# A fused early-fusion block on one core: softmax subtraction moved from GpSimd to VectorE, first-norm rows moved the other way, the attention steps written out

## What is computed

```python
h = concatenate([tok(x), txt], axis=1)            # 64 x 113 x 128
n = layernorm(h)                                  # "first norm"
q, k, v = split(n @ Wq, n @ Wkv)                  # 8 heads of 64
scores = einsum("bqhd,bkhd->bhqk", q * 0.125, k).astype(bfloat16)
probs  = softmax(scores)                          # bfloat16
h = h + (einsum(probs, v).astype(bfloat16) @ Wo + bo)
n2 = layernorm(h)
h = h + shared_swiglu(n2) + sum of the 3 chosen of 16 experts, weighted
```

## Time and profile before

| what | value |
|---|---|
| median of 3 runs (lowest, highest) | 949.9 us (947.1, 950.74) |
| the profiled execution, its span | 947.45 us, 945.5 us |
| busy share of the span: PE, DVE, POOL, ACT | 73%, 62%, 70%, 48% |
| mean granted clock of TensorE | 0.882 |
| L498, the subtraction on POOL | 64 times, 109.5 us busy, 1711 ns each |
| L543, the indirect DMAs that send rows, on POOL | 192 times, 199.2 us busy, 1038 ns each |

### The profile page before, as it was taken

How to read it: one execution, slowest core, us unless ns; L and a number is a source line. 1 busy time by engine, 2 the same in 40 slices (tenths; PEclk the granted TensorE clock), 3 DMA queues, 4 the chain that set the end, 5 groups by cost and what they waited for, 6 DMA issues and landing times.

```text
span 945.5 us, 21371 instructions
## 1 busy us (share of the span) xinstructions
PE 688.0 (73%) x6112; PEld 561.4 (59%) x6112; DVE 589.7 (62%) x1667; ACT 452.2 (48%) x1059; POOL 661.4 (70%) x774
## 2 busy tenths in 40 slices
PE   4834999879878798788888885789777777786000
PEld 3623787768767677677677764468555555564000
DVE  1674788887878879778888786534333333333185
ACT  1532887657657667577576653124233332322000
POOL 2474455887878878878788788737777777777542
PEclk9965999999989989989899985789999999999555
DMA  8710000000000000000000000457665655662396
GB/s 276 225 25 12 2 2 9 27 29 15 25 20 22 27 17 25 27 16 24 20 25 25 22 29 31 127 163 221 182 180 176 184 169 178 173 179 81 97 338 192
DMA packets 66478, 85.54 MB, mean 90 GB/s; under 512 B 14118, under 2 KB 59055, under 8 KB 66282
## 3 DMA queue, kind: packets, MB, share of 16 engines
q1 hardware_dynamic: 30212, 34.62, 13.2%
q10 hardware_dynamic: 23680, 27.98, 10.1%
q0 software_dynamic: 12544, 22.44, 7.1%
HBM read 55.44 MB, written 31.85 MB: 92 GB/s over the span
## 4 chain that ended last, share of the span: by engine, by line
issue 25%; POOL 24%; PE 20%; DVE 9%; DMA 8%; ACT 2%; POOLq 1%; DVEq 0%; SPq 0%; ACTq 0%
POOL dispatched L543 7%; POOL expert_rows L556 7%; PE bank L616 6%; POOL s L498 5%; DMA expert_rows<-yb,xs_all 4%; PE bank L700 3%; DMA x2t<-expert_rows 3%; PE bank L663 2%; PE bank L748 1%; PE bank L716 1%; ACT p L914 1%; PE bank L796 1%; POOL rs L510 1%; POOL h L504 1%; DVE h L1281 1%
## 5 line engine op out<-in xcount | busy, mean ns | idle before, releaser
L556 POOL DMA_INDIRECT expert_rows<-yb,xs_all x200 | 194.5, 973 | 74.4 <-issue 54.9
L543 POOL DMA_INDIRECT dispatched<-pay,sloti x192 | 199.2, 1038 | 60.9 <-issue 57.3
L498 POOL TENSOR_TENSOR s<-s,mx 113x904 bf16<-113x904 bf16 x64 | 109.5, 1711 | 46.4 <-DVE mx L1168 45.9
L1269 DVE TENSOR_TENSOR yb<-bank,xs_all 128x256 f32<-128x256 f32 x100 | 42.3, 423 | 145.0 <-DMA expert_rows<-yb,xs_all 141.2
L616 PE MATMUL bank<-xt,wqkv 128*128 128x452 f32 x384 | 116.4, 441 | 1.1 <-DVE xt L1181 0.7
L796 PE MATMUL bank<-xe,kt 128*128 128x256 f32 x400 | 105.7, 387 | 0.2
L951 ACT ACTIVATE xe<-bank 128x256 f32<-128x256 f32 x100 | 38.4, 384 | 137.8 <-PE bank L784 134.4
L805 PE MATMUL bank<-kt,hide 128*128 128x128 f32 x400 | 67.9, 293 | 47.8 <-DVE hide L1259 47.4
L805 PEld LDWEIGHTS bank<-kt,hide 128*128 128x128 f32 x400 | 54.9, 191 | 76.0 <-DVE hide L1259 67.8
L914 ACT ACTIVATE p<-s 113x904 bf16<-113x904 bf16 x64 | 61.2, 957 | 57.1 <-POOL s L498 57.0
L616 PEld LDWEIGHTS bank<-xt,wqkv 128*128 128x128 f32 x384 | 79.2, 224 | 7.2 <-DVE xt L1181 0.9
(11 more groups left out here) (159 smaller groups left out, 1735.5 us busy)
## 6 DMA issues: line engine op xcount, KB each, us to landing
kt<-in_w_ffn ACTq DMA_DIRECT2D x100, 192.0 KB, 2.4
xs_all<-dispatched SPq DMA_DIRECT2D x100, 130.0 KB, 2.2
x2t<-expert_rows SPq DMA_DIRECT2D x16, 672.0 KB
out_h<-h ACTq DMA_DIRECT2D x16, 224.0 KB
x2t<-in_x ACTq DMA_DIRECT2D x4, 864.0 KB, 7.4
x2t<-in_x SPq DMA_DIRECT2D x4, 864.0 KB, 7.6
expert_rows<-yb,xs_all POOLq DMA_INDIRECT x200, 2.6
dispatched<-pay,sloti POOLq DMA_INDIRECT x192, 2.3
```

Source lines behind the costliest of these rows:

```text
L498: nc.gpsimd.tensor_tensor(s16[k % 2][0:T, :, :], s16[k % 2][0:T, :, :], mx[k % 2][0:T, :].unsqueeze(2).to_broadcast([T, H, T]), ALU.subtra ...
L543: pool.indirect_dma_start(out=xs_dram[:, :], out_offset=bass.IndirectOffsetOnAxis(ap=sloti[:, b // GRP, b % GRP, c:c + 1], axis=0), in_=pa ...
L556: pool.indirect_dma_start(out=y_dram[:, :], out_offset=bass.IndirectOffsetOnAxis(ap=xs[slot][:, j, ROW - 1:ROW].bitcast(I32), axis=0), in_ ...
```

## The change

It has four parts. **The steps are written out**: all ten octets are straight-line code, so that all addresses and wait values are constants. **The subtraction of the maximum** moves from GpSimd to VectorE, directly behind the maximum. `s16` gets one more column (114 = `TP`), the maximum is first copied to pairs (`mx2`, 2 equal values per head), and the subtraction runs over pairs of neighbouring elements with the pair of the head repeated 57 times. **Early clearing**: GpSimd clears `pay` and `sloti` at the start of the kernel and no longer between patches and attention, and VectorE clears `pt` as its first work. **The rows of the first norm**, `xn`, are made by GpSimd at the start of its step instead of by VectorE; `first_rs` is split, so that GpSimd adds EPS for an octet when its statistics are there (`first_eps`), and the power (`first_pow`) is taken for octet 0 in the patches, and for octet o+2 at step k = 6 of octet o.

```diff
-        ve1, ve2 = sb("ve1", [128, OCT]), sb("ve2", [128, 2])
+        ve1, ve2 = sb("ve1", [128, B]), sb("ve2", [128, 2])
-        s16 = [sb(f"s16_{i}", [128, H, T], BF16) for i in range(2)]
+        s16 = [sb(f"s16_{i}", [128, H, TP], BF16) for i in range(2)]
+        mx2 = [sb(f"mx2_{i}", [128, H, 2], BF16) for i in range(2)]
...
-            octet(-1)
-            octet(0)
-            with eng.Fori(1, octets - 1) as o:
+            for o in range(-1, octets + 1):
                 octet(o)
-            octet(octets - 1)
-            octet(octets)
...
+            nc.gpsimd.memset(pay[:, :, :, :], 0.0).then_inc(S["rows_set"], 1)
+            nc.gpsimd.memset(sloti[:, :, :, :], NE * CAP + TR).then_inc(S["rows_set"], 1)
             pool.wait_ge(S["tok_in"], 32)
...
                 if o >= 3:
-                    first_rs(o - 3)
+                    first_eps(o - 3)
+                if o == 3:
+                    first_pow(0)
             patch_shift(NOCT - 1, (NOCT - 1) % 2)
-            first_rs(NOCT - 3)
+            first_eps(NOCT - 3)
             pool.wait_ge(S["attn_in"], 96)
-            nc.gpsimd.memset(pay[:, :, :, :], 0.0).then_inc(S["rows_set"], 1)
-            nc.gpsimd.memset(sloti[:, :, :, :], NE * CAP + TR).then_inc(S["rows_set"], 1)
...
             def step(o, k):                       # GpSimd
-                if ok(n):
-                    after(pool, "max_done", n)
-                    nc.gpsimd.tensor_tensor(s16[k % 2][0:T, :, :], s16[k % 2][0:T, :, :],
-                                            mx[k % 2][0:T, :].unsqueeze(2).to_broadcast([T, H, T]), ALU.subtract).then_inc(S["sub_done"], 1)
+                if k == 6 and o + 2 < NOCT:
+                    first_pow(o + 2)
+                if ok(n + 8):
+                    after(pool, "xt_done", n + 8, -1)
+                    nc.gpsimd.tensor_scalar(xn[k % 2][0:T, :], h[0:T, bass.ds(n + 8, 1), :].rearrange("p a d -> p (a d)"),
+                                            mean1[0:T, bass.ds(n + 8, 1)], rs1[0:T, bass.ds(n + 8, 1)],
+                                            ALU.subtract, ALU.mult).then_inc(S["xn_ready"], 1)
...
         def _(dve):
+            for i in range(2):
+                nc.vector.memset(pt[i][:, :, :], 0.0).then_inc(S["pt_zero"], 1)
             dve.wait_ge(S["tok_in"], 32)
...
             def step(o, k):                       # VectorE
-                if ok(n + 8):
-                    after(dve, "xt_done", n + 8, -1)
-                    nc.vector.tensor_scalar(xn[i][0:T, :], row(n + 8), mean1[0:T, bass.ds(n + 8, 1)], rs1[0:T, bass.ds(n + 8, 1)],
-                                            ALU.subtract, ALU.mult).then_inc(S["xn_ready"], 1)
                 if ok(n):
                     after(dve, "s_copied", n)
-                    nc.vector.reduce_max(mx[i][0:T, :], s16[i][0:T, :, :], AX.X).then_inc(S["max_done"], 1)
+                    nc.vector.reduce_max(mx[i][0:T, :], s16[i][0:T, :, 0:T], AX.X).then_inc(S["max_done"], 1)
+                    nc.vector.tensor_copy(mx2[i][0:T, :, :], mx[i][0:T, :].unsqueeze(2).to_broadcast([T, H, 2])).then_inc(S["mx2_done"], 1)
+                    pairs = s16[i][0:T, :, :].rearrange("p h (c two) -> p h c two", two=2)
+                    nc.vector.tensor_tensor(pairs, pairs, mx2[i][0:T, :, :].unsqueeze(2).to_broadcast([T, H, TP // 2, 2]),
+                                            ALU.subtract).then_inc(S["sub_done"], 1)
```

More of the change, by code:

```diff
@@ L449, in _, with first_eps, first_pow @@
             nc.gpsimd.memset(one[:, :], 1.0).then_inc(S["iota_f"], 1)
+            nc.gpsimd.memset(pay[:, :, :, :], 0.0).then_inc(S["rows_set"], 1)
+            nc.gpsimd.memset(sloti[:, :, :, :], NE * CAP + TR).then_inc(S["rows_set"], 1)
             pool.wait_ge(S["tok_in"], 32)
             pool.wait_ge(S["ones_set"], 5)
-            def first_rs(o):
-                after_all(pool, ("ones_set", 5), ("st1_done", o, 1), ("rs1_done", o, 0))
-                nc.gpsimd.tensor_scalar(ve1[0:T, :], mv1[0:T, :, 1], EPS, None, ALU.add).then_inc(S["ve1_done"], 1)
+            def first_eps(o):
+                after(pool, "st1_done", o)
+                nc.gpsimd.tensor_scalar(ve1[0:T, o * OCT:(o + 1) * OCT], mv1[0:T, :, 1], EPS, None, ALU.add).then_inc(S["ve1_done"], 1)
+            def first_pow(o):
                 after(pool, "ve1_done", o)
-                nc.gpsimd.tensor_tensor(rs1[0:T, bass.ds(o * OCT, OCT)], ve1[0:T, :], half[0:T, :], ALU.pow).then_inc(S["rs1_done"], 1)
+                nc.gpsimd.tensor_tensor(rs1[0:T, o * OCT:(o + 1) * OCT], ve1[0:T, o * OCT:(o + 1) * OCT], half[0:T, :],
+                                        ALU.pow).then_inc(S["rs1_done"], 1)
             def patch_scale(o, i):
@@ L491, in step @@
                 n = o * OCT + k
-                if isinstance(o, int) and o == -1 and k in (4, 5):
-                    first_rs(NOCT - 2 if k == 4 else NOCT - 1)
-                if ok(n):
-                    after(pool, "max_done", n)
-                    nc.gpsimd.tensor_tensor(s16[k % 2][0:T, :, :], s16[k % 2][0:T, :, :],
-                                            mx[k % 2][0:T, :].unsqueeze(2).to_broadcast([T, H, T]), ALU.subtract).then_inc(S["sub_done"], 1)
+                if o == -1 and k in (4, 5):
+                    first_eps(NOCT - 2 if k == 4 else NOCT - 1)
+                if k == 6 and o + 2 < NOCT:
+                    first_pow(o + 2)
+                if ok(n + 8):
+                    if k == 0:
+                        after_all(pool, ("ones_set", 5), ("mean1_done", o + 1, 1), ("rs1_done", o + 1, 1))
+                    after(pool, "xt_done", n + 8, -1)
+                    nc.gpsimd.tensor_scalar(xn[k % 2][0:T, :], h[0:T, bass.ds(n + 8, 1), :].rearrange("p a d -> p (a d)"),
+                                            mean1[0:T, bass.ds(n + 8, 1)], rs1[0:T, bass.ds(n + 8, 1)],
+                                            ALU.subtract, ALU.mult).then_inc(S["xn_ready"], 1)
                 if ok(n + 6):
@@ L860, in _ @@
                     scaled(o - 2)
-            act.wait_ge(S["pt_zero"], 3)
+            act.wait_ge(S["pt_zero"], 5)
             def early(g, i):
@@ L1031, in _ @@
             dve.wait_ge(S["rows_set"], 2)
+            nc.vector.memset(bank[5][:, :], 0.0).then_inc(S["pt_zero"], 1)
             for i in range(2):
-                nc.vector.memset(pt[i][:, :, :], 0.0).then_inc(S["pt_zero"], 1)
-            nc.vector.memset(bank[5][:, :], 0.0).then_inc(S["pt_zero"], 1)
-            dve.wait_ge(S["pt_zero"], 3)
+                nc.vector.memset(s16[i][:, :, T:TP], 0.0).then_inc(S["pt_zero"], 1)
+            dve.wait_ge(S["pt_zero"], 5)
             dve.wait_ge(S["iota_f"], 5)
```

13 lines of the change are left out of this document (6 added, 7 removed).

## The result

The kernel became slower. The change takes 958.4 us (median of 4 runs, 957.1 to 964.3) where the kernel before takes 950.3 us (4 runs, 947.1 to 952.4): the ratio is 1.0108, with a 95% interval of 1.0071 to 1.0144. Forecast were 923 us and a range of 908 to 948. The profiled execution took 957.82 us, its span is 955.7 us.

A forecast was written before the change was run, and what follows sets the result against it. No engine was full; GpSimd's step (3.3 us + 1.25 per send) was taken as the bound in octets 1 to 6. -15.6 + 0.6 - 4 - 8 = -27.0 from 947.45 gives 920.4, median 2.45 higher: 923 us, range 908 to 948.

The forecast's parts named there:

- the holding up at L1055: VectorE's small two-input addition, held up by 2.1 us beside GpSimd's subtraction; forecast to go away.
- octets 0 and 7: First and last attention octets: +0.6 us for octet 0, -4 us for octet 7.
- the hand-over: Between patches and attention: early clearing and GpSimd's earlier `xn` start attention sooner, -8 us.
- the new loop: GpSimd's `xn` behind the sends, through PE, ScalarE and VectorE back to GpSimd: 7.7 us with four sends, 6.4 with three.
- Step by step the larger of GpSimd's loop and VectorE's chain: Octets 1 to 6: the longer per step, sum 59.2, taken as 60.7 us an octet, -15.6 us in six.
- VectorE's chain: VectorE's own work per step: 5.4 us without routing, 6.05 after the change, 6.7 to 7.2 in steps k = 1, 3 and 4.
- rival 2: Loop through `xn` wrong, GpSimd keeps up, octets go by VectorE at 53 us each: 878 us, chance 0.03.
- The price of `xn`: Time of the `xn` row on GpSimd, taken as 0.35 us, between 0.22 and 0.45.
- The power in the loop: GpSimd's power for octet o+2, ahead of `xn` from k = 5 to 6: 1.7 us once per octet.
- Rival 3: Waits for `xn` idle PE and its clock falls, octets 1 to 6 +7 us each: 966 us, chance 0.10.
- 1: Rival: VectorE's subtraction runs one element at a time, 1.09 us: 942 us, chance 0.14.
- 4: Rival: octets' gain at GpSimd lost in full to the new wait, only hand-over and octet 7 remain: 939 us, chance 0.12.

The follow-up runs named there:

- e2: The kernel before with only its loop over octets 1 to 6 written out; ratio to the kernel before 0.9973.
- e4: The changed kernel with GpSimd making `xn` one sample earlier, behind `rs2` and ahead of the step's sends; ratio to the kernel before 0.9674.
- e1: The changed kernel with `xn` back on VectorE, ahead of the maximum; ratio to the kernel before 0.9690.
- e12: The changed kernel with `xn` covering only 16 of 128 channels, the rest staying zero; ratio to the kernel before 0.9962.
- e6: The changed kernel with the power for octet o+2 at the end of k = 0 instead of k = 6; ratio to the kernel before 1.0125.
- e7: e4 with the copy to pairs made by a two-input maximum of the row with itself; ratio to the kernel before 0.9667.
- e10: e7 with the power for octet o+2 at the end of k = 0 instead of k = 6; ratio to the kernel before 0.9607.

## Why the prediction was wrong

**Right, with their sizes.** The subtraction on VectorE where nothing holds it up (0.63 us, forecast 0.6), the end of the holding up at L1055 (2.35 us before, 0.22 after), octets 0 and 7, the hand-over in its sum (-8.6, forecast -8), written-out steps at nothing (e2), and that the new loop exists, with every link named. The groups from 200 to 450 us of the changed kernel that answer to the earlier trace rows, and the mis-sized ones (mean in ns behind the comma):

```profile
L1065 DVE TENSOR_TENSOR wz<-wz,eb_sb 113x64 f32<-113x64 f32 x7 | 1.5, 217 | 0.0
```
```profile
L505 POOL TENSOR_SCALAR xn<-h,mean,rs 113x128 f32<-113x128 f32 x30 | 27.2, 906 | 0.9
L1174 DVE TENSOR_TENSOR s<-s,mx 113x912 bf16<-113x912 bf16 x30 | 22.8, 761 | 3.1
L1171 DVE COPY mx<-mx 113x16 bf16<-113x16 bf16 x30 | 9.2, 306 | 3.1
```

**The step that failed** is "Step by step the larger of GpSimd's loop and VectorE's chain". It took VectorE's chain as a length of its own that runs beside the loop. But VectorE's L1188 is a member of both: it stands for the `xt` of the loop (6.4 us an octet, for which the chain of 5.4 us a step has no room), and what stands behind it, up to the next `mv`, comes late with it. The same holds on PE, whose one queue has the transposition that waits for `xn` ahead of the v and the weighting on which VectorE's reciprocal hangs. The prediction had worked out what is queued behind the wait on GpSimd and left out what is queued behind the waits on VectorE and PE. That the place of `xn` makes the loss is shown: with the row ahead of the sends PE no longer waits for it (11.4 us an octet in the change, none in e4), VectorE's wait for `xt` is down to 0.3, and the octet takes 59.3 us. That this is near the 59.2 which the sum had given for the change is chance: that sum was for another order, with other prices. How the loss is put together, step by step, is read from the waits and argued, not separated by a run.

**VectorE's chain was also put too low.** The steps without routing count 6.05 us, those with it up to 7.2, and rival 2 makes an octet of it 53 us. In e1, where no `xn` is on GpSimd and GpSimd waits for `mv` for 15.8 us an octet, the octets take 60.6 us, with only some 2 us more of work for VectorE. One reason is in the two rows above, means of 0.76 and 0.31 us where 0.6 and 0.2 were forecast: both instructions are held up in some steps. (Of the prediction's 5.4 us for a step without routing, 0.60 is a wait for PE at L1195 in the earlier trace rows that was counted as work, so the other terms are short by more.) An estimate of what is left for the series: with `xn` at its measured price in the loop (+0.5 us), and e1's steps, less up to 0.24 us each for `xn`, in the place of VectorE's chain, the larger of the two in each step comes to some 63 to 64 us an octet. The other 3 to 4 of the 67.3 are what no larger-of-two gives; the clock's part is in there.

**The price of `xn`** was mis-sized, 0.35 us forecast and 0.83 measured (mean 0.91), outside both bounds; they came from instructions without two scalars read from memory. e12 shows that it is not what made the loss: with it nearly halved the kernel takes 0.9962 of the kernel before (0.9925 to 1.0000), where 0.97 was forecast of the change. It is not nothing either, some 1.5% of the time against the change.

**The power in the loop** was right in place and price (1.71 us). Moving it away gave 3.1 us an octet in e6, of which 2.0 in its own step.

**Rival 3**, the falling clock, was given 0.10 and said to decide from a mean of 0.75. The mean is 0.90, so it isn't what made the loss by itself. But its mechanism works in single steps: in the octet shown k = 0, 3, 6 and 7 run at 0.70 to 0.83 (k = 0 and 6 in nearly every octet, right behind PE's longest waits for `xn`), and a step at the lower clock cost 0.8 to 1.4 us more where the same step can be compared. Its kernel-wide form was not met; as an amplifier of the loop it was left out of the sum, and the argument "less time leaves less idle time" was wrong, since the waits grew. How the miss divides between the series and the clock isn't settled: the runs without the loop (e4, e7, e10) have a clock of 0.95 to 0.98, so both go together. PE's whole work in octets 1 to 6 took 320.6 us in the change and 306.0 in e4, 2.4 us an octet more, and e4 and e7 have the same octet at 0.97 and 0.95.

**Rivals 1, 2 and 4.** 1 is out, the pairs run at 0.63 us. 2 is out, nothing but a new order goes around the loop, and its 53 us for VectorE were too low. 4 was nearest, in that the octets' gain was lost to the new wait, but it stopped at "in full"; the wait took 28 us more than that.

## What to carry to other kernels

When a step of work is moved to another engine, look where its consumer stands in its own queue: what is queued behind the consumer is late by the same time, and if the producer hangs on that, two chains that each fit into a step are in part added, and taking the longer of them is too little. Work that starts such a loop belongs ahead of the long instructions of its queue (here ahead of the sends, one sample earlier: from 1.0279 to 0.9667 on one chip, in e7), and a rare long instruction belongs in the step in which its engine has nothing to send. Halving the price of the instruction in the loop, without moving it, brought some 1.5%; moving it at its full price brought 4 to 6%.
